# The last eighth of a strip's attention weights: bf16 upper halves and a fourth transposing DMA in place of f32 turns

## The reference

```python
h = jnp.maximum(_layernorm(x, axis=-1), 0.0)
q = h @ Wq.T + bq
k = h @ Wk.T + bk
v = h @ Wv.T + bv
scores = q @ k.T / jnp.sqrt(jnp.asarray(d, q.dtype))
scores = jnp.where(adj > 0, scores, neg)
attention = jax.nn.softmax(scores, axis=-1)
att = attention @ v
x = x + jax.nn.elu(att)
```

## Time and profile before

| | us |
|---|---|
| median of 3 runs | 744.18 |
| lowest, highest | 743.32, 747.09 |
| the profiled execution | 744.26 |
| its span, first to last instruction | 742.4 |

### The profile page before, as it was taken

The page is one execution under the profiler, slowest core; times in us unless marked ns, Lnnn a source line. Parts: engine busy times, 40 slices in busy tenths (PEclk is TensorE's granted clock), DMA queues, the critical chain, the costliest instruction groups (busy, mean ns, idle before and its releaser), DMA issues. The chain is left out here.

```text
span 742.4 us, 18373 instructions
## 1 busy us (share of the span) xinstructions
PE 713.7 (96%) x6269; PEld 604.4 (81%) x6269; DVE 564.3 (76%) x1207; ACT 540.9 (73%) x1091; POOL 454.5 (61%) x388
## 2 busy tenths in 40 slices
PE   7998999999999999999999999977999999999997
PEld 5667888888888888888888878866888888888885
DVE  6967778787887878878788787797978467577572
ACT  4745867778778787787777877897697797797810
POOL 6778799999999999999999998692000000000000
PEclk9999999999999999999999999998999999999999
DMA  7279999998898978979889773973334353442200
GB/s 241 87 226 304 244 281 237 262 263 234 282 257 248 265 232 281 256 245 265 235 280 255 247 164 86 180 92 87 78 88 87 73 93 68 92 95 64 41 11 13
DMA packets 192783, 132.51 MB, mean 178 GB/s; under 512 B 173536, under 2 KB 180192, under 8 KB 184544
## 3 DMA queue, kind: packets, MB, share of 16 engines
q1 hardware_dynamic: 192000, 131.63, 66.4%
q10 hardware_dynamic: 576, 0.26, 0.1%
q0 software_dynamic: 160, 0.00, 0.0%
HBM read 71.04 MB, written 18.89 MB: 121 GB/s over the span
## 5 line engine op out<-in xcount | busy, mean ns | idle before, releaser
L802 ACT ACTIVATE scores<-scores,neg_max 128x1024 f32<-128x1024 f32 x128 | 146.0, 1142 | 48.2 <-DVE neg_max L937 48.2
L950 DVE TENSOR_TENSOR low<-scores 128x1024 bf16<-128x1024 f32 x96 | 135.5, 1412 | 38.4 <-ACT scores L802 38.4
L1219 PE MATMUL spare<-v_parts,hiT 128*128 128x256 bf16 x768 | 161.7, 274 | 0.0
L931 DVE CUSTOM_DVE_ANT_0 scores<-ps_s,mask_both 128x1024 f32<-128x1024 f32 x128 | 155.9, 1218 | 0.4 <-POOL mask_both L365 0.4
L365 POOL TENSOR_SCALAR mask_both<-mask_bytes 128x2048 bf16<-128x2048 uint8 x64 | 151.8, 2372 | 5.4 <-POOL mask_bytes L360 0.4
L360 POOL TENSOR_SCALAR mask_bytes<-adj_both 128x2048 uint8<-128x2048 int32 x64 | 149.8, 2359 | 3.8 <-DMA adj_both<-in_adj 2.9
L1215 PE MATMUL spare<-v_parts,lowT 128*128 128x128 bf16 x768 | 144.8, 220 | 3.4 <-DMA lowT<-low 3.4
L816 ACT ACTIVATE hiT<-spare 128x512 bf16<-128x512 bf16 (+1 forms) x128 | 102.4, 801 | 35.0 <-PE spare L1189 32.5
L1678 PE MATMUL ps_x<-q_parts,over_k 128*128 128x258 bf16 x1024 | 117.7, 276 | 3.9 <-issue 3.9
L1678 PEld LDWEIGHTS ps_x<-q_parts,over_k 128*128 128x128 fp8e4 x1024 | 100.3, 99 | 19.8 <-issue 4.1
L1154 PE MATMUL ps_s<-k_hi,q_strip 128*128 128x512 f32 x256 | 112.4, 439 | 2.2 <-PEq L83 1.9
(11 more groups left out here) (181 smaller groups left out, 1297.9 us busy)
## 6 DMA issues: line engine op xcount, KB each, us to landing
adj_both<-in_adj SPq DMA_DIRECT2D x64, 1024.0 KB, 5.3
mask_bytes_dram<-mask_bytes SPq DMA_DIRECT2D x32, 512.0 KB, 2.8
x_sb<-in_x SPq DMA_DIRECT2D x8, 256.0 KB, 7.6
out<-res SPq DMA_DIRECT2D x32, 64.0 KB, 1.5
lowT<-low SPq DMA_TRANSPOSE x96, 4.8
mask_both<-s_row_dram SPq DMA_DIRECT2D x2, 768.0 KB, 7.1
over_k<-mask_bytes_dram SPq DMA_TRANSPOSE x16, 4.6
scores<-mask_bytes_dram SPq DMA_TRANSPOSE x16, 4.5
```

The costliest lines, as they stand in the source:

```text
L802: nc.scalar.activation(sc, sc, ACT.Exp, bias=neg_max[:, bn:bn + 1], accum_out=row_sum[:, bn, k:k + 1]).then_inc(exp_done, 1)
L931: nc.vector.tensor_tensor_reduce(out=scores[bn % 2][:, part(k)], in0=ps_s[k % 2][:], in1=mask[bn % 2][:, part(k)], scale=1.0, scalar=LOWES ...
L950: nc.vector.tensor_tensor(low[k][:], p, high_half(p), ALU.subtract).then_inc(low_done, 1)
L1219: last = nc.tensor.matmul(ps_a[:], high, v_parts[:, t, :, :], start=first, stop=final)
```

## The change

For chunk 7, the last eighth of the strip, the first way of turning takes the place of the second. Chunk 6 stays as it was.

- TensorE turns the bf16 upper halves of its four tiles, against the bf16 identity, into the first half of the same PSUM bank. ScalarE's second `copy_pT` reads them as bf16.
- VectorE's second `turned_low` goes. A new `last_low` subtracts the upper halves from the 512 words of chunk 7, both operands in SBUF, into a new buffer `low_last`. It stands behind `low_part(s, b, 2)`.
- SyncE turns `low_last` with a fourth transposing DMA a strip (`turn_last_low`) into `pT_low[1]`, behind `turn_low` 2 and ahead of the mask store and the loads.
- TensorE multiplies the rest of chunk 7 not with chunk 7 but with the last chunk of the order (chunk 5), in the next period, and waits for the new DMA there. Two waits for `pT_low` become waits for `pT_high`.

```diff
                         act.wait_ge(t_done, TURNS * s + i + 1)
                         wait(act, pv_done, 8 * (s - 1) + i + 1)
-                        nc.scalar.activation(pT_high[i][:], ps_t[i % 3][:], ACT.Copy).then_inc(pT_ready, 1)
+                        out = ps_t[0][:] if i == 0 else ps_t[1][:].bitcast(BF16)[:, 0:512]
+                        nc.scalar.activation(pT_high[i][:], out, ACT.Copy).then_inc(pT_ready, 1)
...
+                    def turn_last_low(c, b):
+
+                        s = 4 * c + b
+                        sp.wait_ge(last_low_done, s + 1)
+                        sp.sem_inc(sp_gate, 1)
+                        if not (isinstance(s, int) and s == 0):
+
+                            sp.wait_ge(pv_done, 8 * s)
+                            sp.sem_inc(sp_gate, 1)
+                        sp.dma_start(pT_low[1][:].rearrange("p (t f) -> p t f", f=D), low_last[:],
+                                     transpose=True).then_inc(last_lowT_in, 16)
...
                         turn_low(c, b, 2)
+                        turn_last_low(c, b)
...
+                    def last_low(s, b):
+
+                        dve.wait_ge(exp_done, 4 * s + 1)
+                        wait(dve, last_lowT_in, 16 * s)
+                        p = scores[b % 2][:, N - 512:N]
+                        nc.vector.tensor_tensor(low_last[:], p, high_half(p), ALU.subtract).then_inc(last_low_done, 1)
...
                         elif ahead:
-                            turned_low(s, 0)
+                            turned_low(s)
                             low_part(s, b, 1)
                             add_mask(s + 1, bn, 2)
-                            turned_low(s, 1)
                             low_part(s, b, 2)
+                            last_low(s, b)
                             add_mask(s + 1, bn, 3)
                             find_max(s + 1, bn)
...
+                            if i == 0:
+                                turned = nc.tensor.transpose(ps_t[0][:, D * t:D * t + D], scores[b % 2][:, col:col + D], ident[:])
+                            else:
+                                turned = nc.tensor.transpose(ps_t[1][:].bitcast(BF16)[:, D * t:D * t + D],
+                                                             last_high[:, D * t:D * t + D], ident_half[:])
...
+                        if i == NC - 1:
+                            pe.wait_ge(last_lowT_in, 16 * s + 16)
...
+                        if i == NC - 1:
+
+                            times_low(pT_low[1][:, D * n:D * n + D], T - 4 + n)
+                        if not first and i != 1:
+                            times_low(rest, t)
```

More of the change, by code:

```diff
@@ L580, in build @@
                 lowT = [sb(c2, f"lowT{k}", [D, 8, D], BF16) for k in range(3)]
+                low_last = sb(c2, "low_last", [D, 512], BF16)
                 acc_sb = sb(c2, "acc_sb", [D, 2, D], F32)
@@ L674, in _ @@
                     sp.wait_ge(low_done, 3 * T)
+                    sp.wait_ge(last_low_done, T)
                     for b in range(4):
@@ L1181, in turn_high @@
                             wait(pe, hiT_ready, 4 * s)
-                        elif u < 3:
-                            pe.wait_ge(pT_low_ready, 2 * s + u)
+                        elif u == 1:
+                            pe.wait_ge(pT_low_ready, s + 1)
+                        elif u == 2:
+                            pe.wait_ge(pT_ready, 2 * s + 2)
                         else:
@@ L1193, in wait_for_part @@
                         j = PV_ORDER[i]
-                        if i < 2:
-                            pe.wait_ge(pT_low_ready, 2 * s + i + 1)
+                        if i == 0:
+                            pe.wait_ge(pT_low_ready, s + 1)
+                        elif i == 1:
+                            pe.wait_ge(pT_ready, 2 * s + 2)
                         else:
@@ L1212, in tile_times_v, with times_low @@
                             high, rest = hiT[j // 2][:, D * (t % 8):D * (t % 8) + D], lowT[j // 2][:, t % 8, :]
-                        def times_low():
+                        def times_low(rest, t):
                             return nc.tensor.matmul(ps_a[:, 0, :], rest, v_parts[:, t, 0, :], start=False, stop=False)
-                        if not first:
-                            times_low()
+                        if i == NC - 1:
+                            times_low(pT_low[1][:, D * n:D * n + D], T - 4 + n)
+                        if not first and i != 1:
+                            times_low(rest, t)
                         last = nc.tensor.matmul(ps_a[:], high, v_parts[:, t, :, :], start=first, stop=final)
                         if first:
-                            last = times_low()
+                            last = times_low(rest, t)
                         return last
```

9 lines of the change are left out of this document (5 added, 4 removed).

## The result

| | before | after |
|---|---|---|
| median, us (6 runs each) | 744.12 | 805.72 |
| lowest, highest | 742.88, 747.09 | 803.49, 807.42 |
| span of the profiled execution | 742.4 | 805.6 |
| ratio after / before, 95% interval | | 1.0828 (1.0804 to 1.0853) |

The change costs 8.3%. The forecast was 761 us with a range from 752 to 785, so the time lies outside the range. It lies 2 us from the 808 of the first rival, to which the prediction gave a chance of 0.12.

A forecast was written before the change was run, and what follows sets the result against it. The prediction took VectorE and ScalarE, waiting on each other, to set 13.28 us a strip, with GpSimd nearly full. Adding 28 x 0.60 = 16.8 us for last_low, 742.4 + 16.8 + 1.86 = 761.1 us; range 752 to 785.

The forecast's parts named there:

- first rival: Behind low part 2, GpSimd's waiting mask half goes before last_low: 2.29 us a strip, 808 us; chance 0.12.
- What bounds the kernel: In the attention strips, VectorE and ScalarE releasing each other set 13.28 us a strip; TensorE alone would take 13.13.
- The circle of VectorE and ScalarE: Row maximum releases ScalarE's exponentials, ScalarE's first copy releases VectorE's pT_low: 6.6 plus 6.7 us make 13.28 a strip.
- TensorE counted at 0: Cheaper bf16 turns free 0.22 us of TensorE a strip, 6.9 over 32 strips, counted as 0 us of time.
- One strip taken for all: The strip starting at 240.42 was stepped through, and its 0.60 us delay was expected to repeat in strips 2 to 29.
- Low part 2 gains nothing by its earlier issue: On VectorE, low part 2 is issued at 243.31 instead of 243.91 but still starts work at 244.40, behind a mask half.
- The fourth DMA at 0: SyncE's extra transposing DMA lands 4.8 us after issue, before its products need it: price 0.
- the prediction's own TensorE round: TensorE's time for one strip after the change, 13.13 - 0.22 = 12.91 us.
- last_low at 0.60: Undisturbed on VectorE behind low part 2, last_low costs 0.60 us a strip: 28 x 0.60 = 16.8 us.
- Who gets the turn behind low part 2: The uncertain step: VectorE keeps its turn, so last_low goes before GpSimd's waiting second mask half, at 0.60 us a strip.
- The price of the rival: If the mask half goes before last_low, add_mask 3 starts 2.29 us later each strip: 28 x 2.29 = 64.1 us.
- all three of its signs: Signs of GpSimd going first: last_low 2.4 us long, maxima 15.6 apart, GpSimd waiting over 2 us for att_exp.

The follow-up runs named there:

- The TensorE part alone: Changed kernel with bf16 turns kept but last_low, the fourth transposing DMA and the four products with the rest of chunk 7 left out: 743.58 us, ratio 0.9997.
- one operand: Changed kernel with last_low reading one SBUF operand, scaling the 512 words instead of subtracting, so the rest of chunk 7 is not computed: 758.58 us, ratio 1.0189.
- without waits between: Changed kernel with last_low's two waits taken out from between it and low part 2: 807.02 us, ratio 1.0840.
- cut low part: Kernel before with VectorE's low part 2 written as two instructions of 512 elements, nothing else changed: 794.99 us, ratio 1.0679.
- other form: Changed kernel with last_low and the three low parts written as SCALAR_TENSOR_TENSOR in place of TENSOR_TENSOR: 806.21 us, ratio 1.0829.

## Why the prediction was wrong, point by point

- **What bounds the kernel: right.** The circle of VectorE and ScalarE sets the strip. Whatever was added to VectorE within it appeared in the spacing of the maxima: 0.5 us where last_low ran undisturbed, 2.29 where it did not. Behind the maximum it cost almost nothing.
- **TensorE counted at 0: right.** The TensorE part alone gives a ratio of 0.9997.
- **One strip taken for all: not quite, and without harm.** In the kernel before, the strip of the prediction stands for three of four. In the first of each loop round low part 1 takes 1.45 us and low part 2 its undisturbed 1.21, and the strip still takes 13.28. In the changed kernel these strips take 15.5 us, like the others.
- **Low part 2 gains nothing by its earlier issue: right.** Its work still began only when the first mask half ended (273.69 - 1.22 = 272.47, the half's end at 272.62). It is drawn as 2.29 instead of 1.70, which is the 0.60 of the missing pT_low spent standing.
- **The fourth DMA at 0: right for itself.** It lands 2.4 us after issue, not the 4.8 taken from the earlier trace rows, and nothing waited for it. TensorE waited for the transposing DMAs of the low parts for 14.7 us in 100 to 460 us, in strips that had 15.57 - 12.91 = 2.66 us of slack by the prediction's own TensorE round.
- **last_low at 0.60: right for an undisturbed one** (0.68 long at 521.73; 758.6 us with one operand).
- **"Who gets the turn behind low part 2": wrong**, and this is the whole error. The step took the earlier trace rows over the earlier trace rows, VectorE keeps its turn, and explained the slip in the earlier trace rows by a gap of 0.06 us. The runs show the other way in all 28 strips, without waits between and with a cut instruction. The term was 0.60 where 2.29 was measured; 28 x 1.69 = 47.3 us, and 761.1 + 47.3 = 808.4.
- **The price of the rival: right.** 2.29 us a strip was forecast from the mask half's 1.90 and the 0.14 us by which VectorE resumes before GpSimd's record ends; 15.57 - 13.28 = 2.29 was measured, with all three of its signs (last_low 2.4, maxima 15.6, GpSimd waiting over 2 us for att_exp).

The evidence for a better chance was in the trace of before, and I stopped one step short of it. These rows lie 8 us behind the earlier trace rows, the same two lines L344 and L340 of the kernel before, in order of time:

```profile
490.87 1.53 DVE L344 SCALAR_TENSOR_TENSOR q_parts<-adj_both,q_parts 128x512 f32<-128x512 f32 x1
...
490.36 1.50 POOL L340 TENSOR_TENSOR q_parts<-q_parts 128x516 bf16<-128x516 f32 x1
491.81 1.49 POOL L340 TENSOR_TENSOR q_parts<-q_parts 128x516 bf16<-128x516 f32 x1
```

L340 is issued at 490.36, waits until the L344 before has ended, and then runs its 1.05 us while the next L344, issued at 490.87, is stretched from 0.68 to 1.53. Here GpSimd got in between two L344, against the one place on which the step rested. The next L344, issued at 492.32, is stretched to 1.53 in the same way. With three places for it and one against it, the rival should have had at least half of the chance. That its 808 us came within 2.3 us of the measurement is no luck: the price was worked out from the mechanism that the runs show.

What stays open is why VectorE keeps its turn in a few places. The last strip but one of after is such a place, VectorE and then GpSimd in order of time:

```profile
521.73 0.68 DVE L967 TENSOR_TENSOR low_last<-scores 128x512 bf16<-128x512 f32 x1
...
520.72 1.93 POOL L747 TENSOR_SCALAR adj_both<-x_sb,minus_mean,rstd 128x128 f32<-128x128 f32 x1
```

L747 had been waiting for 1.0 us when last_low was issued, and last_low went first. It is so too in this strip of the run without waits between (last_low at 521.30, 0.68 us, L747 issued at 520.28), and the cut low part of the kernel before kept its turn against L731 (508.17, 0.69 us, L731 issued at 507.68), the line that had slipped in at the earlier trace rows. The runs exclude the waits between, the form of VectorE's instruction and its length as what decides. GpSimd's instruction isn't it alone either, since L340 got in at one place and not at another. I have no theory that covers all places.

## What to carry to other kernels

Where GpSimd works on SBUF all the time, count each VectorE instruction with two SBUF operands as a possible wait for a whole GpSimd instruction, and two of them in a row as a likely one, unless a trace shows that GpSimd is idle there. Put an instruction that reads PSUM between them, or place the second behind the point on which others wait: one moved line was worth 57 us here. And look at all places of a trace where two such instructions follow each other before one is taken as the rule.

## What the runs showed of the chip that I had not expected

- A GpSimd instruction that waits gets in between two VectorE instructions that follow each other without any gap or wait: 28 of 28 mask halves behind low part 2, in the changed kernel and in each of the three runs that kept such a pair (cut low part, no waits between, other form). Cutting one VectorE instruction of 1024 elements into two of 512 cost 50 us in 744.
- The engine that waits resumes about 0.14 us before the record of the other ends (273.55 against 273.69, 275.30 against 275.45), in both directions. The first number of each pair is an estimate: the end less the undisturbed duration.
- Relief of an engine that locks another out needn't pay: with one GpSimd instruction less, three strips of four took 12.80 us and the fourth 14.83, since an earlier mask half came 0.08 us ahead of low part 1. A delay of 0.24 us on ScalarE where a round of the loop begins seems to decide who comes first.
- A transposing DMA of 128 x 512 bf16 lands 2.4 us after issue, one of 128 x 1024 4.1 us in the same kernel; they hold the issuing queue for 1.19 and 1.34 us (medians), almost alike.
